# Edge counts of a four-layer graph network: place registers loaded by fours, and the narrow one-hots of twelve steps compared in one instruction

## Chip, cores and metric

One core of one Trainium2 chip runs the whole program in one launch. The metric is device time in microseconds (us): the median of three runs of the kernel before is 5613.37 us (5609.27 to 5640.14). One more run was recorded by the hardware profiler; every row below comes from it.

## The reference, cut to what matters

Four graph layers run one after the other on 3125 nodes with 64 features and the same 100,000 edges, which come sorted by `dst`: an attention layer (8 heads), two mean aggregations, an edge-weighted aggregation, and a second attention layer with a feed-forward part. The first two layers need, for every pair of nodes, nothing but how many edges join them, for instance:

```python
scores = leaky_relu(alpha_src[src] + alpha_dst[dst], 0.2)
att = exp(clip(scores, -2.0, 2.0))
att_sum = segment_sum(att, src, N)
out = segment_sum(h[dst] * (att / att_sum[src])[:, :, None], src, N)
...
msg_sum = segment_sum(x[src], dst, n)      # mean aggregation, twice
mean = msg_sum / maximum(deg, 1.0)[:, None]
```

Both sums over edges can be written as products with a dense table counts[dst, src], the number of edges from src to dst. The change lies wholly in the stage that builds this table.

## The kernel before

**Sizes.** The edges are cut into G = 800 groups of P = 125. The `dst` nodes are cut into V = 125 windows of D = 25 nodes. A step is one (group, window) pair that shares edges; there are KV = 800 + 125 - 1 = 924 steps, in order of window. For each edge of a step the stage `order_edges` has worked out `src_code` (the src's place, 0 to 124, inside its own block of 125 nodes) and `pair_code` (0 to 649: which of 26 columns per dst, 25 of them blocks of 125 src nodes, and which of the 25 dst nodes; a code outside marks an edge of another window).

**One step** (class `Count`). VectorE (DVE) makes two one-hot tables in bf16 by comparing an iota row with one value per partition: the wide one, `pair_hot`, 125 x 650 (line 484), and the narrow one, `src_hot`, 125 x 125 (line 485). TensorE (PE) multiplies them: 125 edges contracted, narrow one-hot as the weights, wide one-hot as the moving operand, in two halves of 325 columns (line 525), and adds onto a 125 x 650 fp32 table in PSUM. There are 12 places (UV = 12) for each one-hot; DVE may refill a place once PE has counted the step that used it (`count_ready`), PE may use it once `hot_ready` says so.

**One window.** Which PSUM table a step adds to is data: a window has some 7.4 steps on average and there are four PSUM places (SLOTS = 4) used in turn. The place of each step is in the row `fine.slot`, and the number of places that must have been cleared before a pair of steps may write is in `fine.turn` (one value per two steps). ScalarE (ACT) waits until a window is complete, copies 125 x 650 out (line 500), clears the place (line 503), and the SyncE queue (SP) writes the window to HBM in two DMAs (line 473), with DEEP = 6 windows in flight.

**What sets PE's order.** The PE program is straight-line. At the start of each round of 12 steps it loads registers from SBUF (`values`, line 460): twelve `slot` values in one instruction and six `turn` values in another. Then for each step it waits for `hot_ready`, for each second step it waits for `slot_free` against a `turn` register (line 523), and issues two matmuls, each preceded by a register operation that forms the PSUM address. 924 steps make 77 rounds.

Before the stage, PE and ACT compute score rows while DVE already makes the first 12 pairs of one-hots; after it comes a barrier, and the attention layer reads the table back from HBM. Elsewhere in the program (class `Unpack`, line 201) PE, ACT and DVE load registers four at a time (AT_LOAD = 4).

Of the kernel before, what the change touches and what calls it, by code (L numbers as in the profile page):

```python
# [21 lines left out]
BF16 = mybir.dt.bfloat16  # L22
F16 = mybir.dt.float16
I32 = mybir.dt.int32
ALU = mybir.AluOpType
# [4 lines left out]
P = 125  # L30
# [8 lines left out]
V = N // D  # L39
KV = G + V - 1  # L40
UV = 12
CW = 26 * D
FAR = 1.0e30
AT_ONCE = 2
# [6 lines left out]
SLOTS = 4  # L51
# [78 lines left out]
def over(ap, shape):  # L130
    return ap.to_broadcast(list(shape))
# [174 lines left out]
def order_edges(nc, m):  # L306


    with ExitStack() as stack:
# [25 lines left out]
        def _(dve):  # L335
# [37 lines left out]
            own(v.tensor_tensor(t.window_f[:, :], m.step_iota[:, 0:KV], group[:, :], ALU.subtract))  # L373
            own(v.tensor_scalar(first[:, :], t.window_f[0:P, :], float(CW), -MIDDLE, ALU.mult, ALU.add))

            own(v.tensor_scalar(row[:, 0:HALF], t.window_f[0:1, 1:KV:2], 1.0, None, ALU.add))
            own(v.tensor_copy(t.turn[:, :], row[:, 0:HALF]))
            own(v.tensor_scalar(row[:, :], t.window_f[0:1, :], 1.0 / SLOTS, None, ALU.mult))
            own(v.tensor_copy(t.slot[:, :], row[:, :]))
            own(v.tensor_copy(row[:, :], t.slot[:, :]))  # L380
# [56 lines left out]
class Count:  # L437
# [7 lines left out]
    def __init__(self, nc, s, m):  # L445
        self.nc, self.m = nc, m
        used = DEEP * CW + 3 * N
        hot = m.arena[0:P, used:used + UV * (CW + P) // 2].bitcast(BF16)
        self.pair_hot = hot[:, 0:UV * CW].rearrange("p (i c) -> p i c", i=UV)
        self.src_hot = hot[:, UV * CW:].rearrange("p (i c) -> p i c", i=UV)  # L450
        self.zeros = s.sb("zeros", [P, CW // 2], BF16)
        self.sum = [m.arena[0:P, i * CW:(i + 1) * CW].rearrange("p (a c) -> p a c", a=2) for i in range(DEEP)]
        self.ps = s.ps("count_ps", (128, SLOTS, 2, 512))
        self.sum_out = s.sems("sum_out", DEEP)
        self.blank, self.hot_ready, self.count_ready = s.sem("blank"), s.sem("hot_ready"), s.sem("count_ready")
        self.evicted, self.slot_free = s.sem("evicted"), s.sem("slot_free")

    def values(self, engine, table, k, n, most):

# [18 lines left out]
    def dve(self, dve):  # L478
        nc, m, v = self.nc, self.m, self.nc.vector

        for k in range(KV):
            if k >= UV:
                dve.wait_ge(self.count_ready, k - UV + 1)
            v.tensor_scalar(self.pair_hot[:, k % UV, :], m.code_iota[:, :], m.fine.pair_code[:, k:k + 1], None, ALU.is_equal)  # L484
            v.tensor_scalar(self.src_hot[:, k % UV, :], m.node_iota[:, :], m.fine.src_code[:, k:k + 1], None,  # L485
                            ALU.is_equal).then_inc(self.hot_ready, 1)

    def act(self, act):

# [15 lines left out]
    def pe(self, pe, tables):  # L505
        nc, m = self.nc, self.m

        pe.wait_ge(self.blank, 1)
        pe.wait_ge(tables.scores_taken, 1)
        pe.wait_ge(tables.rows_copied, 2 * tables.chunks)  # L510
        for i in range(SLOTS):
            for c in range(2):
                last = nc.tensor.matmul(self.ps[0:P, i, c, 0:CW // 2], self.zeros[:, 0:P], self.zeros[:, :],
                                        start=True, stop=True, skip_group_check=True)
            last.then_inc(self.slot_free, 1)

        for k in range(KV):
            if k % UV == 0:
                slots = self.values(mybir.EngineType.PE, m.fine.slot, k, UV, SLOTS - 1)
                turns = self.values(mybir.EngineType.PE, m.fine.turn, k // 2, UV // 2, V)  # L520
            pe.wait_ge(self.hot_ready, k + 1)
            if k % 2 == 0:
                pe.wait_ge(self.slot_free, turns[k % UV // 2])
            for c in range(2):
                last = nc.tensor.matmul(self.ps[0:P, bass.ds(slots[k % UV], 1), c, 0:CW // 2].rearrange("p a f -> p (a f)"),  # L525
                                        self.src_hot[:, k % UV, :], self.pair_hot[:, k % UV, c * (CW // 2):(c + 1) * (CW // 2)],
                                        start=False, stop=True, skip_group_check=True)
            last.then_inc(self.count_ready, 1)

# [1762 lines left out]
def program(nc, io, out):  # L2292
    m = Memory()
    with ExitStack() as stack:
# [29 lines left out]
        with ExitStack() as first:  # L2324
# [11 lines left out]
            with ExitStack() as held:  # L2336
                m.arena = held.enter_context(nc.sbuf_tensor("arena", [128, HELD * AT_ONCE * V // W * CW], F32))
                m.held = Counts(nc, held, m)
                with ExitStack() as layer0:
                    def layer0_sb(name, shape, dt=F32):  # L2340
                        return layer0.enter_context(nc.sbuf_tensor(name, shape, dt))
                    m.wt0, m.at0, m.merge = layer0_sb("wt0", [F, HF]), layer0_sb("at0", [F, 2 * H]), layer0_sb("merge", [F, H, F])
                    m.node_iota = layer0_sb("node_iota", [P, P], F16)
                    m.group_iota = layer0_sb("group_iota", [ROWS, RUNS])
                    m.far_past, m.far_left = layer0_sb("far_past", [P, W, H]), layer0_sb("far_left", [P, W, H])
                    with ExitStack() as early:
                        def early_sb(name, shape, dt=F32):
                            return early.enter_context(nc.sbuf_tensor(name, shape, dt))
                        m.src_rows, m.dst_rows = early_sb("src_rows", [ROWS, EACH], I32), early_sb("dst_rows", [ROWS, EACH], I32)
                        m.code_iota = early_sb("code_iota", [P, CW], F16)  # L2350
                        m.fine = Memory()
                        m.step_iota16 = early_sb("step_iota16", [ROWS, KV], F16)
                        m.fine.window_f = early_sb("fine_window_f", [128, KV])
                        m.fine.src_code, m.fine.pair_code = (early_sb(f"fine_{n}", [P, KV]) for n in ("src_code", "pair_code"))
                        m.fine.slot, m.fine.turn = (early_sb(f"fine_{n}", [1, k], I32) for n, k in (("slot", KV), ("turn", HALF)))
                        m.fine.counted = early_sb("fine_counted", [1, V], I32)
                        set_up(nc, m, io)
                        order_edges(nc, m)
                        count_and_tables(nc, m)
                    m.gathered = layer0_sb("gathered", [P, W, F])  # L2360
                    attend(nc, m, "l0")
                    finish_layer0(nc, m)
                    m.acc = m.sums
                count_sum(nc, m, "l1a", 0, with_tiles=True)
                with ExitStack() as extra:
                    m.held.grow(nc, extra)
                    finish_mean(nc, m, "l1a_end", m.sage1[:, :], m.rows[:, 0:F], "hidden")
                    count_sum(nc, m, "l1b", 1)
                finish_mean(nc, m, "l1b_end", m.sage2[:, :], m.rows[:, F:2 * F], "last")
# [41 lines left out]
```

## Time and profile before

| | |
|---|---|
| median of three runs | 5613.37 us |
| the profiled run, its own time | 5605.08 us |
| its span, first to last instruction | 5603.3 us |
| DVE busy over the span | 3211.7 us (57%) |
| PE matmul busy over the span | 3079.5 us (55%) |
| granted TensorE clock, mean of the span | 0.712 |
| count stage, first to last matmul of line 525 | 103.0 to 588.9 us |

Busy times overlap between engines, and a stage ends when its last engine does; so the share of an engine over the whole span does not say what the count stage waits for. Idle time is read from the rows of the stage itself: a row's bracket gives the idle time of its engine just before it and what ended it. "issue" stands for time in which the engine waited for nothing that the profile shows as work; loads of registers are such time, and they are listed only where one asks for their source line (engine names with a q, as PEldq, are the sequencer's own instructions).

### The profile page before, as it was taken

The page shows a single profiled execution, that of the slowest core. Times are in us where ns is not written, and L with a number is a line of the kernel's source. Part 1 is how long each engine was busy: PE and PEld are TensorE (multiplying, and loading weights), DVE is VectorE, ACT ScalarE, POOL GpSimd, SP SyncE. Part 2 cuts the span into 40 slices and gives each one's busy share as a digit, 9 for nine tenths or more (in the row PEclk, how much of TensorE's full clock was granted, in tenths as well). Part 3 has the DMA queues.
Part 4 walks back from the last instruction along what each step waited for, and adds up shares of the span by engine and source line. Part 5 has one row for each costly group of instructions (what it writes and reads, how often), then busy time and mean ns, then how long its engine had stood idle before and what let it go on. Part 6 is the DMA issues. An engine that isn't in the chain of part 4 may idle for free. (4 is left out here: it accounts for less than half of the span.)

```text
span 5603.3 us, 46575 instructions
## 1 busy us (share of the span) xinstructions
PE 3079.5 (55%) x11765; PEld 1927.7 (34%) x11765; DVE 3211.7 (57%) x5607; ACT 1827.1 (33%) x2737; POOL 1842.8 (33%) x1787
## 2 busy tenths in 40 slices
PE   5777688877777776885334432441101543433564
PEld 3555333322222222553223332441001433333552
DVE  6999799999999997102132111112211854556676
ACT  1333688888888885000000000000101111111200
POOL 0000222100000000001777777754775066665200
PEclk7888899999999998997555555555555555555556
DMA  1222666544444444984214222102111011111011
GB/s 38 83 85 85 170 186 191 162 118 120 119 120 123 118 116 112 211 181 99 48 40 98 45 48 44 43 17 37 31 27 29 15 37 32 37 31 30 4 42 32
DMA packets 381011, 448.82 MB, mean 80 GB/s; under 512 B 182902, under 2 KB 249365, under 8 KB 379839
## 3 DMA queue, kind: packets, MB, share of 16 engines
q1 hardware_dynamic: 328477, 390.50, 27.0%
q0 software_dynamic: 52288, 55.34, 5.1%
q8 instruction: 117, 1.92, 0.2%
q14 instruction: 129, 1.06, 0.1%
HBM read 351.39 MB, written 94.23 MB: 80 GB/s over the span
## 5 line engine op out<-in xcount | busy, mean ns | idle before, releaser
L889 PE MATMUL l_sum_ps<-arena,sums 125*65 125x500 f32 (+1 forms) x2600 | 1146.0, 580 | 295.8 <-DVE arena L783 272.1
L1808 POOL DMA_INDIRECT l_rows<-table,tile_src x782 | 772.1, 987 | 508.5 <-issue 229.6
L1219 POOL DMA_INDIRECT l_rows<-hidden_rows,tile_src x782 | 806.4, 1031 | 304.9 <-issue 233.9
L772 DVE SCALAR_TENSOR_TENSOR arena<-arena,far_past 125x750 f32<-125x750 f32 (+1 forms) x800 | 859.7, 1114 | 16.5 <-DMA arena<-score_rows 16.5
L1272 PE MATMUL l_acc_ps<-l_rows,l_hot 128*125 x1612 | 389.6, 388 | 718.6 <-issue 683.3
L818 ACT ACTIVATE arena<-arena,far_left 125x750 f32<-125x750 f32 (+1 forms) x800 | 713.0, 939 | 186.0 <-DVE arena L772 186.0
L783 DVE SCALAR_TENSOR_TENSOR arena<-arena,l_turned 125x1500 f32<-125x1500 f32 (+1 forms) x400 | 711.6, 1779 | 47.9 <-ACT arena L823 47.3
L2002 PE MATMUL l_sum_ps<-l_rows,l_hot 128*128 x1962 | 482.4, 425 | 439.5 <-issue 302.1
L889 PEld LDWEIGHTS l_sum_ps<-arena,sums 125*65 125x65 f32 x2600 | 331.6, 138 | 1045.0 <-issue 534.6
L1272 PEld LDWEIGHTS l_acc_ps<-l_rows,l_hot 128*125 128x125 f32 x1612 | 367.1, 313 | 742.2 <-issue 740.3
L2002 PEld LDWEIGHTS l_sum_ps<-l_rows,l_hot 128*128 128x128 f32 x1962 | 437.7, 327 | 483.0 <-issue 480.7
L823 ACT ACTIVATE arena<-arena 125x1500 f32<-125x1500 f32 (+1 forms) x400 | 596.7, 1492 | 0.0
L1923 DVE SCALAR_TENSOR_TENSOR acc<-acc,l_factor,l_sum_ps 128x65 f32 x981 | 275.9, 281 | 549.3 <-DMA found_rows<-l_w_last_i 344.9
L525 PE MATMUL l0tab_count_ps<-arena 125*125 125x325 bf16 x1848 | 348.8, 353 | 140.2 <-DVE arena L485 136.3
L484 DVE TENSOR_SCALAR arena<-code_iota,fine_pair_code 125x650 bf16<-125x650 f16 x924 | 356.6, 386 | 54.5 <-PE l0tab_count_ps L525 54.3
L1311 ACT ACTIVATE l_end_dense_sb<-l_end_ps_t 128x500 f32<-128x500 f32 (+1 forms) x7 | 3.7, 542 | 1168.9 <-PE l_end_ps_t L1297 1168.9
L744 POOL TENSOR_TENSOR gathered<-gathered,arena 125x384 f32<-125x384 f32 (+1 forms) x12 | 28.4, 2363 | 1068.0 <-DVE arena L796 1068.0
L1236 DVE TENSOR_TENSOR l_rows<-l_rows,l_attr 128x512 f32<-128x512 f32 x98 | 68.0, 694 | 517.2 <-DMA l_rows<-hidden_rows,tile_src 482.4
L525 PEld LDWEIGHTS l0tab_count_ps<-arena 125*125 125x125 bf16 x1848 | 282.3, 157 | 207.0 <-issue 161.2
L2049 ACT ACTIVATE l_step_att<-l_att 128x8 f32 x981 | 176.9, 208 | 469.7 <-issue 393.7
L1230 DVE TENSOR_TENSOR l_hot<-tile_rel,node_row 128x1000 f32<-128x1000 f32 x101 | 120.5, 1194 | 338.9 <-DMA arena<-counts 305.4
L485 DVE TENSOR_SCALAR arena<-node_iota,fine_src_code 125x125 bf16<-125x125 f16 x924 | 230.8, 250 | 0.0
(464 smaller groups left out, 2738.3 us busy)
## 6 DMA issues: line engine op xcount, KB each, us to landing
l_turned<-turned_counts SPq DMA_DIRECT2D x225, 328.1 KB
arena<-counts SPq DMA_DIRECT2D x17, 2843.8 KB
counts<-arena SPq DMA_DIRECT2D x125, 284.4 KB
l_turned<-turned_counts SPq DMA_DIRECT2D x75, 382.8 KB
l_attr<-edge_attr_in SPq DMA_DIRECT2D x97, 256.0 KB
arena<-counts SPq DMA_DIRECT2D x75, 328.1 KB
turned_counts<-l_turned SPq DMA_DIRECT2D x75, 328.1 KB
arena<-score_rows SPq DMA_DIRECT2D x24, 732.4 KB
```

The lines of the kernel that those rows point to most:

```text
L484: v.tensor_scalar(self.pair_hot[:, k % UV, :], m.code_iota[:, :], m.fine.pair_code[:, k:k + 1], None, ALU.is_equal)
L525: last = nc.tensor.matmul(self.ps[0:P, bass.ds(slots[k % UV], 1), c, 0:CW // 2].rearrange("p a f -> p (a f)"), self.src_hot[:, k % UV, :], ...
L772: last = v.scalar_tensor_tensor(scores(k)[:, i, :], rows[:, 1, i, :], m.far_past[:, w, h:h + 1], rows[:, 0, i, :], ALU.add, ALU.max)
L783: v.scalar_tensor_tensor(scores(k), scores(k), LOWEST, over(turned_counts(k).unsqueeze(1), (P, PAIR, n * P)), ALU.max, ALU.mult).then_inc( ...
L818: last = nc.scalar.activation(here, here, ACT.Relu, scale=-1.0, bias=m.far_left[:, w, h:h + 1])
L823: nc.scalar.activation(scores(k), scores(k), ACT.Exp, scale=-1.0).then_inc(raised, 1)
L889: last = nc.tensor.matmul(sum_ps[0:F + 1, c, 0:hi - lo], h_one[:, w, :], z[k % ZS][:, lo:hi], start=(w == 0), stop=(w == W - 1))
L1219: pool.indirect_dma_start(rows[:, b % RING, t, :], None, m.hidden_rows[:, :], bass.IndirectOffsetOnAxis(ap=m.tile_src[:, k:k + 1], axis=0) ...
L1272: last = nc.tensor.matmul(nodes[:, bass.ds(window, 1), :].rearrange("p a f -> p (a f)"), hot[r % HOTS][:, j, :], flat[:, bass.ds(place, 1) ...
L1808: pool.indirect_dma_start(rows[:, t % RING3, :], None, m.table3[:, :], bass.IndirectOffsetOnAxis(ap=m.tile_src[:, t:t + 1], axis=0)).then_ ...
L1923: v.scalar_tensor_tensor(window, window, factor[:, k:k + 1], sum_ps[g % 4][:, i * (F + 1):(i + 1) * (F + 1)], ALU.mult, ALU.add).then_inc( ...
L2002: last = nc.tensor.matmul(sum_ps[g % 4][:, i * (F + 1):(i + 1) * (F + 1)], hot[g % 3][:, i, :, :].rearrange("p h j -> p (h j)"), rows[:, b ...
```

## The change

- The PE program loads four `slot` values at each fourth step (one instruction), and four `turn` values at each sixteenth (three at the last). `fine.turn` holds one value per four steps, that of the last of the four, and PE waits for `slot_free` once per four steps, ahead of them.
- DVE no longer compares the narrow one-hot step by step. One two-operand comparison makes those of twelve steps: a table `node_step` (node number, repeated for twelve steps, fp16, made once) against twelve `src_code` values, now kept in fp16 and read again for each node. The result lies node by node with the twelve steps side by side, so the 125 weights of one step are 12 elements (24 bytes) apart. There is room for three such groups (NARROW = 36 steps); group g + 1 is compared in the middle of group g.
- PE waits once per twelve steps for `narrow_ready`. The wide one-hots and the matmuls' shapes and number stay.

```diff
--- before.py
+++ after.py
@@ -39,6 +39,7 @@
 V = N // D
 KV = G + V - 1
 UV = 12
+NARROW = 3 * UV
 CW = 26 * D
 FAR = 1.0e30
 AT_ONCE = 2
@@ -373,8 +374,8 @@
             own(v.tensor_tensor(t.window_f[:, :], m.step_iota[:, 0:KV], group[:, :], ALU.subtract))
             own(v.tensor_scalar(first[:, :], t.window_f[0:P, :], float(CW), -MIDDLE, ALU.mult, ALU.add))
 
-            own(v.tensor_scalar(row[:, 0:HALF], t.window_f[0:1, 1:KV:2], 1.0, None, ALU.add))
-            own(v.tensor_copy(t.turn[:, :], row[:, 0:HALF]))
+            own(v.tensor_scalar(row[:, 0:KV // AT_LOAD], t.window_f[0:1, AT_LOAD - 1:KV:AT_LOAD], 1.0, None, ALU.add))
+            own(v.tensor_copy(t.turn[:, :], row[:, 0:KV // AT_LOAD]))
             own(v.tensor_scalar(row[:, :], t.window_f[0:1, :], 1.0 / SLOTS, None, ALU.mult))
             own(v.tensor_copy(t.slot[:, :], row[:, :]))
             own(v.tensor_copy(row[:, :], t.slot[:, :]))
@@ -445,15 +446,18 @@
     def __init__(self, nc, s, m):
         self.nc, self.m = nc, m
         used = DEEP * CW + 3 * N
-        hot = m.arena[0:P, used:used + UV * (CW + P) // 2].bitcast(BF16)
+        hot = m.arena[0:P, used:used + (UV * CW + NARROW * P) // 2].bitcast(BF16)
         self.pair_hot = hot[:, 0:UV * CW].rearrange("p (i c) -> p i c", i=UV)
-        self.src_hot = hot[:, UV * CW:].rearrange("p (i c) -> p i c", i=UV)
+        self.src_hot = hot[:, UV * CW:].rearrange("p (a c i) -> p a i c", a=NARROW // UV, i=UV)
+        self.node_step = s.sb("node_step", [P, P, UV], F16)
+        self.node_step_ready = s.sem("node_step_ready")
         self.zeros = s.sb("zeros", [P, CW // 2], BF16)
         self.sum = [m.arena[0:P, i * CW:(i + 1) * CW].rearrange("p (a c) -> p a c", a=2) for i in range(DEEP)]
         self.ps = s.ps("count_ps", (128, SLOTS, 2, 512))
         self.sum_out = s.sems("sum_out", DEEP)
         self.blank, self.hot_ready, self.count_ready = s.sem("blank"), s.sem("hot_ready"), s.sem("count_ready")
         self.evicted, self.slot_free = s.sem("evicted"), s.sem("slot_free")
+        self.narrow_ready = s.sem("narrow_ready")
 
     def values(self, engine, table, k, n, most):
 
@@ -478,12 +482,21 @@
     def dve(self, dve):
         nc, m, v = self.nc, self.m, self.nc.vector
 
+        v.tensor_copy(self.node_step[:, :, :], over(m.node_iota[:, :].unsqueeze(2), (P, P, UV))).then_inc(self.node_step_ready, 1)
+        dve.wait_ge(self.node_step_ready, 1)
+
+        def narrow(a):
+            v.tensor_tensor(self.src_hot[:, a * UV % NARROW // UV, :, :].rearrange("p i c -> p c i"), self.node_step[:, :, :],
+                            over(m.fine.src_code[:, a * UV:(a + 1) * UV].unsqueeze(1), (P, P, UV)), ALU.is_equal
+                            ).then_inc(self.narrow_ready, 1)
+        narrow(0)
         for k in range(KV):
             if k >= UV:
                 dve.wait_ge(self.count_ready, k - UV + 1)
-            v.tensor_scalar(self.pair_hot[:, k % UV, :], m.code_iota[:, :], m.fine.pair_code[:, k:k + 1], None, ALU.is_equal)
-            v.tensor_scalar(self.src_hot[:, k % UV, :], m.node_iota[:, :], m.fine.src_code[:, k:k + 1], None,
+            v.tensor_scalar(self.pair_hot[:, k % UV, :], m.code_iota[:, :], m.fine.pair_code[:, k:k + 1], None,
                             ALU.is_equal).then_inc(self.hot_ready, 1)
+            if k % UV == UV // 2 and k // UV + 1 < KV // UV:
+                narrow(k // UV + 1)
 
     def act(self, act):
 
@@ -515,15 +528,18 @@
             last.then_inc(self.slot_free, 1)
 
         for k in range(KV):
+            if k % AT_LOAD == 0:
+                slots = self.values(mybir.EngineType.PE, m.fine.slot, k, AT_LOAD, SLOTS - 1)
+            if k % AT_LOAD ** 2 == 0:
+                turns = self.values(mybir.EngineType.PE, m.fine.turn, k // AT_LOAD, min(AT_LOAD, (KV - k) // AT_LOAD), V)
+            if k % AT_LOAD == 0:
+                pe.wait_ge(self.slot_free, turns[k // AT_LOAD % AT_LOAD])
             if k % UV == 0:
-                slots = self.values(mybir.EngineType.PE, m.fine.slot, k, UV, SLOTS - 1)
-                turns = self.values(mybir.EngineType.PE, m.fine.turn, k // 2, UV // 2, V)
+                pe.wait_ge(self.narrow_ready, k // UV + 1)
             pe.wait_ge(self.hot_ready, k + 1)
-            if k % 2 == 0:
-                pe.wait_ge(self.slot_free, turns[k % UV // 2])
             for c in range(2):
-                last = nc.tensor.matmul(self.ps[0:P, bass.ds(slots[k % UV], 1), c, 0:CW // 2].rearrange("p a f -> p (a f)"),
-                                        self.src_hot[:, k % UV, :], self.pair_hot[:, k % UV, c * (CW // 2):(c + 1) * (CW // 2)],
+                last = nc.tensor.matmul(self.ps[0:P, bass.ds(slots[k % AT_LOAD], 1), c, 0:CW // 2].rearrange("p a f -> p (a f)"),
+                                        self.src_hot[:, k % NARROW // UV, k % UV, :], self.pair_hot[:, k % UV, c * (CW // 2):(c + 1) * (CW // 2)],
                                         start=False, stop=True, skip_group_check=True)
             last.then_inc(self.count_ready, 1)
 
@@ -2351,8 +2367,8 @@
                         m.fine = Memory()
                         m.step_iota16 = early_sb("step_iota16", [ROWS, KV], F16)
                         m.fine.window_f = early_sb("fine_window_f", [128, KV])
-                        m.fine.src_code, m.fine.pair_code = (early_sb(f"fine_{n}", [P, KV]) for n in ("src_code", "pair_code"))
-                        m.fine.slot, m.fine.turn = (early_sb(f"fine_{n}", [1, k], I32) for n, k in (("slot", KV), ("turn", HALF)))
+                        m.fine.src_code, m.fine.pair_code = early_sb("fine_src_code", [P, KV], F16), early_sb("fine_pair_code", [P, KV])
+                        m.fine.slot, m.fine.turn = (early_sb(f"fine_{n}", [1, k], I32) for n, k in (("slot", KV), ("turn", KV // AT_LOAD)))
                         m.fine.counted = early_sb("fine_counted", [1, V], I32)
                         set_up(nc, m, io)
                         order_edges(nc, m)
```

## Rows read from the trace of the kernel before

**Rows 1.** Waits, count stage: engine, line, waited-for, us, times, longest

```profile
PEld l0tab_count_ps L525 <- issue: 161.2, 78, 3.5
PE l0tab_count_ps L525 <- DVE arena L485: 136.3, 65, 3.2
DVE arena L484 <- PE l0tab_count_ps L525: 54.3, 53, 11.3
```

**Rows 2.** Busy time by stretch: length, PE, PEld, DVE, ACT, POOL, clock, DMA, GB/s

```profile
103.00:589.00 486.00, 348.56 (x1848) 282.23 (x1848) 439.10 (x1824) 174.93 (x245) 0.00 (x0) 0.86 0.27 84
750.00:2150.00 1400.00, 1108.31 (x3101) 392.17 (x3100) 1356.38 (x1122) 1200.33 (x1166) 137.57 (x96) 0.98 0.48 134
```

**Rows 3.** Timeline, PE and weight loads: start, us, line, shape, count, [idle before]

```profile
301.29 3.85 PE L525 MATMUL l0tab_count_ps<-arena 125*125 125x325 bf16 x24 [2.82 <-DVE arena L485]
...
307.43 0.77 PE L525 MATMUL l0tab_count_ps<-arena 125*125 125x325 bf16 x4 [2.28 <-DVE arena L485]
...
301.29 3.59 PEld L525 LDWEIGHTS l0tab_count_ps<-arena 125*125 125x125 bf16 x24 [3.07 <-issue]
...
301.29 0.38 PEld L525 LDWEIGHTS l0tab_count_ps<-arena 125*125 125x125 bf16 x3 [3.07 <-issue]
...
173.92 6.41 PE L525 MATMUL l0tab_count_ps<-arena 125*125 125x325 bf16 x23 [3.20 <-DVE arena L485]
```

**Rows 4.** Register loads by line, ns min/median/max: 297:308, then whole span

```profile
L460 PEldq TENSOR_LOAD <-fine_slot x2: 851/1046/1242, 298.1 to 304.8; - x2
L460 PEldq TENSOR_LOAD <-fine_turn x2: 1062/1534/2005, 299.0 to 306.1; - x2
...
L460 PEldq TENSOR_LOAD <-fine_slot x77: 843/868/3384, 97.8 to 582.9; - x77
L460 PEldq TENSOR_LOAD <-fine_turn x77: 818/1438/2218, 101.3 to 584.2; - x77
L460 ACTq TENSOR_LOAD <-fine_counted x32: 291/308/510, 96.7 to 587.1; - x32
...
L201 PEldq TENSOR_LOAD <-words x246: 14/333/700, 3985.4 to 5399.0; - x123
```

**Rows 5.** Timeline, DVE: start, us, engine, line, shape, [idle before]

```profile
304.14 0.39 DVE L484 TENSOR_SCALAR arena<-code_iota,fine_pair_code 125x650 bf16<-125x650 f16 x1
304.44 0.25 DVE L485 TENSOR_SCALAR arena<-node_iota,fine_src_code 125x125 bf16<-125x125 f16 x1
304.60 0.39 DVE L484 TENSOR_SCALAR arena<-code_iota,fine_pair_code 125x650 bf16<-125x650 f16 x1
...
25.05 3.05 DVE L348 TENSOR_SCALAR arena<-step_iota,order_finish 100x924 f16<-100x924 f16 x8
```

**Rows 6.** DVE instructions by line, ns min/median/max: one operand, then two

```profile
L242 DVE TENSOR_SCALAR h<-h x4: 993/993/994, 70.8 to 3805.7; 125x1600 f32<-125x1600 f32 x4
...
L348 DVE TENSOR_SCALAR arena<-step_iota,order_finish x8: 453/454/461, 25.1 to 27.7; 100x924 f16<-100x924 f16 x8
...
L228 DVE TENSOR_TENSOR l0tab_cen<-x,l0tab_mean x1: 1826/1826/1826, 61.7 to 61.7; 125x1600 f32<-125x1600 f32 x1
```

**Rows 7.** Weight loads by line, ns min/median/max: far apart, then side by side

```profile
L1966 PEld LDWEIGHTS l_far_ps<-ident,l_rows x104: 132/173/279, 3954.8 to 5202.2; 128*64 128x64 f32 x96, 128*14 128x14 f32 x8
...
L2184 PEld LDWEIGHTS l3end_heads_t<-ident,acc x200: 108/173/178, 5411.1 to 5523.6; 128*64 128x64 f32 x100
```

**Rows 8.** ACT and SP queue by line, ns min/median/max

```profile
L500 ACT ACTIVATE arena<-l0tab_count_ps x125: 712/713/716, 107.1 to 589.2; 125x650 f32<-125x650 f32 x125
...
L503 ACT ACTIVATE l0tab_count_ps<-l0tab_zeros x121: 715/715/717, 107.8 to 575.7; 125x650 f32<-125x650 bf16 x121
...
L473 SPq DMA_DIRECT2D counts<-arena x250: 298/309/1482, 107.8 to 590.3; - x125
```

**Rows 9.** Timeline at the stage's start: start, us, engine, line, count, [idle before]

```profile
102.96 5.90 PEld L525 LDWEIGHTS l0tab_count_ps<-arena 125*125 125x125 bf16 x24 [3.27 <-issue]
...
103.81 0.39 DVE L484 TENSOR_SCALAR arena<-code_iota,fine_pair_code 125x650 bf16<-125x650 f16 x1 [11.28 <-PE l0tab_count_ps L525]
```

## Prediction

> **What bounds the kernel now.** I read the waits of the count stage first, then its busy time by stretch, then one round on the timeline, and last the sequencer's own instructions by source line. The stage takes 486.0 us from 103 to 589 us, 8.7% of the span [rows 2]; 77 rounds of 12 steps, so 6.31 us a round. No engine is full in it: DVE is busy 439 of 486 us, PE's matmuls 349, ACT 175 [rows 2]. The waits name two things: PE's weight loads stood still 161.2 us for "issue", in 78 places, that is once a round, while DVE waited 54.3 us for PE, in 53 places [rows 1]. The 136 us put down to DVE on the matmul rows are the same gaps seen from the other side: one round shows it. From 301.29 us PE issues 24 matmuls; the next come at 307.43, 6.14 us later [rows 3]. Its two register loads begin at 304.8 and 306.1 us and take 1.24 and 1.06 us [rows 4]; in the round before they began at 298.1 and 299.0 and took 0.85 and 2.01, and the weight load at 301.29 stood idle 3.07 us [rows 3, 4]. DVE could not have helped: with all twelve places full it waits for PE's first step. So the round is PE's: load the registers, then issue 24 matmuls, and nothing on PE lies beside the loads.
>
> The terms of a round at full clock come from these rows. Three weight loads in a row span 0.38 us, the last one 0.13 of it, so one matmul is issued each (0.38 - 0.133)/2 = 0.1235 us. All 24 weight loads span 3.59 us: 3.46 up to the start of the last, less 23 x 0.1235 = 2.84, leaves 0.62 for the five waits of line 523 in between, 0.124 each. Around the loads: from the start of a last weight load to the next first one are 3.07 + 0.13 = 3.20 us, of which 2.86 are the two loads; the other 0.34 are a wait and a matmul's issue (0.247) and some 0.05 for each load; with 0.36 in the other round I take 0.06 a load. At half clock a round's matmuls are the array's: 23 of them span 6.41 us, 0.27 each, 6.5 for 24 [rows 3].
>
> **Register loads by fours and one wait per four steps.** Per round go the 12-value load (median 0.868 us) and the six-value load (median 1.438, least 0.818), some 2.3 us by medians, plus 0.12 [rows 4]. In come 3 loads of `slot` and 0.75 of `turn`, each of four values. PE's loads of four in another stage take 0.333 us (median of 246), and ACT's loads of four in this very stage 0.308 (median of 32, longest 0.51) [rows 4]. 3.75 x (0.333 + 0.06) = 1.47 us. Of six waits three remain, 0.37 us; the new wait for the narrow one-hots adds 0.12. Issue stays: 24 x 0.1235 = 2.96. PE's round: 2.96 + 0.37 + 0.12 + 1.47 = 4.93 us. The bounds: if all loads hid behind queued matmuls the round would be 3.46; with a load of four at what the shortest six-value load took here (0.818 + 0.06) it is 2.96 + 0.49 + 3.29 = 6.74. I take 4.93, since two engines agree on a load of four. Queued behind a blocked `slot_free` wait are up to eight matmuls; it asks for a place given back some three windows, 22 steps, earlier, so it should stay satisfied.
>
> The Trainium skill speaks against loading in small pieces: Runtime: NRT & Kernel Launch (section Instruction fetch mechanics) gives about 200 ns for each register. By it four would cost 0.8 us, a round 3.45 + 3.75 x 0.86 = 6.7, and the stage would lengthen by some 30 us. The trace disagrees: four take 0.333 us, twelve 0.868 [rows 4].
>
> **The narrow one-hots.** DVE now starts a wide comparison 0.30 us before the narrow one and a narrow one 0.16 before the next wide one [rows 5]; 12 x 0.46 = 5.52 us a round. Two wide ones in a row are not in the trace, but eight comparisons of 924 elements span 3.05 us at 0.454 each, so the next starts 0.08 us before the end of one [rows 5, 6]; 0.385 - 0.085 = 0.30 holds for wide after wide. The comparison of 1500 elements with two 16-bit operands has no row. Two-operand work on fp32 takes 1.826 us for 1600 elements, 1.72 for 1500. One-operand work takes 0.993 us for 1600 fp32 and 0.454 for 924 16-bit elements; less some 0.16 and 0.21 of fixed time that is 0.52 and 0.26 ns an element, so 16 bits halve it [rows 6]. Bounds: 0.6 us (at the one-operand 16-bit rate) and 1.72; I take half the fp32 rate, 0.94, or 0.85 start to start. DVE's round is then 12 x 0.30 + 0.85 = 4.45 us, between 4.1 and 5.2. It stays under PE's 4.93 unless near the upper end, and twelve places are enough to ride over the lump in the middle of a group. DVE's new work at the start (making `node_step` and the first group, under 3.5 us) lies in the 11.28 us that it waited there [rows 9]: nothing; without that cover, 3.5 us once.
>
> **Weights 24 bytes apart.** Weight loads whose weights lie 292 bytes apart (line 1966) have a median of 173 ns, like those side by side (line 2184) for the same 64 columns [rows 7]. Both are mostly from the slow level of the clock, so at the fast level the cost isn't shown. I take nothing. A load may even grow to 4.93/24 = 0.205 us a matmul before it is seen. The Trainium skill speaks against this layout as well: SBUF — State Buffer (the note on 16-byte cachelines) says that each access in a new line pays a penalty, with eight bf16 as the free distance; twelve is beyond it. It gives no size; the row shows none.
>
> **The clock.** In the stage the granted clock is 0.86 of full, so 28% of it at 1.2 GHz, where PE stood idle 2.5 to 3.5 us in each round; from 750 to 2150 us, with PE busy 79% of the time in small gaps, it is 0.98 [rows 2, 3]. The idle pieces shrink to 0.4 to 0.8 us, so I take 10% at the low level: 1/(0.9/4.93 + 0.1/6.5) = 5.05 us a round.
>
> **Others.** ACT needs 2 x 0.71 us and a quarter of 0.31 a window, 1.5 of the 3.1 us that a window will last; SP's two issues are under 1 us a window in most cases [rows 4, 8]. Edits of `order_edges` are a few tenths of a microsecond. At the start the first loads end earlier, 3.27 us of idle before 102.96 [rows 9]: a gain of 2 us (0 to 2.6).
>
> **Sum.** 77 x 5.05 = 389 us in place of 486: 97 us, with the start 99 us. The profiled run of 5605.1 us (1.8 outside its span) would be 5506; it lies 8.3 below the median, so the median of 5613.4 becomes 5514.
>
> **Rivals.**
> - PE's round under 4.9 us, with loads hidden in part behind the queue: DVE's 4.45 then binds, 343 us, 5468 at the least. For it: at half clock the array is slower than issue, so matmuls queue up and a load can pass beside them. Against: at full clock PE's weight loads start evenly at 0.1235 us apart, and the gap after them is the full length of the loads [rows 3, 4].
> - The narrow comparison at one element per cycle, 1.72 us: DVE's round 3.6 + 1.63 = 5.23, 403 us, 5528. For: the fp32 rows. Against: 16-bit rows at double rate.
> - The clock swings as now: 1/(0.72/4.93 + 0.28/6.5) = 5.28, 407 us, 5532; at the low level throughout 6.5, 500 us, 5625, no change.
> - Slower: on PE in this stage a load costs by the instruction and not by the value. For: six and twelve values have nearly the same least time, 0.818 and 0.843. Then 6.74 a round, 519 us, less 2: 5644. It decides from (6.31 - 3.45)/3.75 - 0.06 = 0.70 us a load.
> - Strided weights at double the recorded 0.133 us, with nothing hidden: 24 x 0.266 = 6.4, 491 us, 5617, no change; it decides from 0.263. Three times would be 9.6, 250 us slower.
> - The change doesn't do what it says: loads by fours cost nearly what they cost now. No change.
>
> **Chances.** Forecast 0.65; lower 0.05; one element per cycle 0.10; clock as now 0.06, low throughout 0.02; slower loads 0.07; strided weights 0.04, half of it slower; no effect 0.01. A difference of 0.5% (28 us) is about what a measurement of this kernel can tell. Faster 0.65 + 0.05 + 0.10 + 0.06 = 0.86, same 0.05, slower 0.09. The range takes in the first four cases: 5488 (a round of 4.7) to 5560.
>
> **What would show it.** Right: rounds of the 24 matmuls near 5 us, PE idle pieces of 0.4 to 0.9 us three or four times a round, register loads of four near 0.33 us, a comparison of 125 x 1500 of 0.94 us 77 times, clock over 0.93 in the stage, DVE waiting for PE. Wrong: loads of four over 0.7 us, weight loads over 0.2 us at full clock, or PE waiting for DVE with a comparison of 1.7 us. All later stages should only shift.

## The result, and the profile after

The changed kernel's median is 5537.5 us (5530.4 to 5544.8, four runs) against 5617.7 (5609.3 to 5640.1, four runs): ratio 0.9853, 95% interval 0.9824 to 0.9881, 80 us less. A second set of runs (e5 below) gave 5550.0 against 5628.8, ratio 0.9863 (0.9844 to 0.9882), 79 us less. The forecast, made from a median of 5613.4 for the kernel before, was 5514 in a range of 5488 to 5560; 99 us less were expected.

Lines of the page of the changed kernel (part 1, and two rows of the 40 slices):

```profile
PE 3147.2 (57%) x11765; PEld 2053.9 (37%) x11765; DVE 3153.6 (57%) x4761; ACT 1829.5 (33%) x2737; POOL 1839.6 (33%) x1787
...
PE   6997888787877777893253424250002533434564
...
PEclk8998999999999998996565555555555555555556
```

Its busy time by stretch, columns as in [rows 2]; first the count stage (to 505 us, where it reached 589 before), then the neighbour sums of the mean aggregations and the last attention layer, which the change doesn't touch:

```profile
103.00:505.00 402.00, 401.56 (x1839) 401.34 (x1837) 378.75 (x983) 175.59 (x246) 0.00 (x0) 1.00 0.33 102
...
2135.00:2507.00 372.00, 326.06 (x1488) 206.62 (x1488) 36.59 (x73) 13.29 (x33) 1.73 (x3) 0.94 0.90 181
...
3789.00:5347.00 1558.00, 539.76 (x2276) 478.42 (x2276) 751.36 (x1859) 233.15 (x1036) 818.42 (x828) 0.50 0.14 26
```

PE and its weight loads are now busy in all 402 us, at a granted clock of 1.00; before it was 349 of 486 us at 0.86 [rows 2]. The waits of the stage, columns as in [rows 1], agree: the 161 us in which weight loads stood still are gone, and of the stage itself nearly nothing waits but ACT:

```profile
ACT arena L513 <- PE l0tab_count_ps L541: 228.8, 125, 7.5
...
DVE arena L496 <- PE l0tab_count_ps L541: 8.3, 4, 7.9
```

The stage by source line (duration ns min/median/max, first and last start). Line 541 was 525, 489 is the new comparison, 496 the wide one, 464 the register loads [rows 4, 6]:

```profile
L541 PEldq FUSED_REGOPS  x1848: 46/46/51, 99.9 to 501.1; - x185
L541 PEld LDWEIGHTS l0tab_count_ps<-arena x1848: 291/312/322, 100.0 to 504.0; 125*125 125x125 bf16 x185
L541 PE MATMUL l0tab_count_ps<-arena x1848: 329/382/637, 100.0 to 504.2; 125*125 125x325 bf16 x185
...
L464 PEldq TENSOR_LOAD <-fine_slot x231: 327/332/978, 96.9 to 499.7; - x116
L464 PEldq TENSOR_LOAD <-fine_turn x58: 325/329/2258, 97.5 to 496.2; - x58
...
L489 DVE TENSOR_TENSOR arena<-l0tab_node_step,fine_src_code x77: 930/933/941, 87.7 to 492.2; 125x1500 bf16<-125x1500 f16 x77
```

From the first to the last matmul are 404.2 us, 5.25 a round; it was 485.9. A weight load is recorded with 312 ns where it had 133 [rows 3]. And the last register operation starts at 501.1 us, 3.1 us ahead of the last matmul (before: 588.7 and 588.9): PE's sequencer, the part that executes waits, register loads and issues, has run ahead, and what it has issued stands in the queue as work for the array, the part that multiplies. On the timeline the matmuls follow without a gap, 0.218 us apart (6.49 less the last one's 0.38 is 6.11 us for 28):

```profile
299.78 6.49 PE L541 MATMUL l0tab_count_ps<-arena 125*125 125x325 bf16 x29
```

Where the time went: the stage's first weight load starts 3.0 us earlier (99.99 against 102.96 [rows 9]), the stage is 81.7 us shorter, and the attention layer behind it starts 84.7 us earlier. The two profiled spans differ by only 60.2 us, as two later stages that the change doesn't touch were longer in this one: the second and third stretch above, 372 and 1558 us, were 360 and 1542. The profiled run of before was 13 us under its median and this one 7 over; the medians, 80 us apart, show the stage's gain.

### The profile page after: what moved, and what is told of

The parts are those of the page before. It is cut to its first block and busy times, and to the rows that moved or that the text cites. A ratio compares the mean times of both kernels' runs of the same rounds, so it can differ in the third digit from the quotient of the medians.

```text
span 5543.1 us, 45633 instructions
## 1 busy us (share of the span) xinstructions
PE 3147.2 (57%) x11765; PEld 2053.9 (37%) x11765; DVE 3153.6 (57%) x4761; ACT 1829.5 (33%) x2737; POOL 1839.6 (33%) x1787
## 5 line engine op out<-in xcount | busy, mean ns | idle before, releaser
L1288 PE MATMUL l_acc_ps<-l_rows,l_hot 128*125 x1612 | 387.8, 390 | 717.8 <-issue 700.6
L541 PE MATMUL l0tab_count_ps<-arena 125*125 125x325 bf16 x1848 | 404.6, 383 | 0.7 <-PE l0tab_count_ps L526 0.7
L541 PEld LDWEIGHTS l0tab_count_ps<-arena 125*125 125x125 bf16 x1848 | 404.4, 313 | 1.2 <-issue 1.2
L496 DVE TENSOR_SCALAR arena<-code_iota,fine_pair_code 125x650 bf16<-125x650 f16 x924 | 326.9, 390 | 26.4 <-PE l0tab_count_ps L541 8.3
L769 POOL COPY arena<-arena 125x750 f32<-125x750 f32 (+1 forms) x100 | 123.6, 1237 | 306.3 <-PE l_count_ps L894 238.4
```

Source lines behind the costliest of these rows:

```text
L541: last = nc.tensor.matmul(self.ps[0:P, bass.ds(slots[k % AT_LOAD], 1), c, 0:CW // 2].rearrange("p a f -> p (a f)"), self.src_hot[:, k % NA ...
L1288: last = nc.tensor.matmul(nodes[:, bass.ds(window, 1), :].rearrange("p a f -> p (a f)"), hot[r % HOTS][:, j, :], flat[:, bass.ds(place, 1) ...
```

## Experiments

e1 to e4 ran on another chip, on which the kernel before takes 5333.9 us (5328.2 to 5340.3) and not 5617; the last attention layer is some 185 us shorter in the runs there. The edge-weighted aggregation is some 90 us shorter there. So between chips only the count stage is compared (time from its first to its last matmul), and ratios go by runs of the kernel before on the experiment's own chip. The stage of the kernel before was profiled on one chip only; its 485.9 us stand for the others too, and the ratios bear that out (e3: 62 us of the stage, 63 us by the medians). Rows of an experiment are of its main matmul line and its line of register loads; means of register loads are worked out from all those of PE in the stage, and a distance between matmuls is the median over the stage.

**e1: weights 8 bytes apart.**

```diff
-NARROW = 3 * UV
+NU, NARROW = 4, 36
-... "p (a c i) -> p a i c", a=NARROW // UV, i=UV
+... "p (a c i) -> p a i c", a=NARROW // NU, i=NU
-            if k % UV == UV // 2 and k // UV + 1 < KV // UV:
-                narrow(k // UV + 1)
+            if k % NU == NU // 2 and (k // NU + 1) * NU < KV:
+                narrow(k // NU + 1)
```

The same replacement stands in `narrow`, in `node_step` and in PE's wait for `narrow_ready`, which now comes every four steps.

> The changed kernel with the narrow one-hots compared by four steps, so that a step's weights lie 8 bytes apart and not 24. In the changed kernel a matmul starts each 0.218 us (before: 0.142 at full clock) and PE is never idle, 24 x 0.218 = 5.23 us a round. Theory A (what counts is how many of the weights share a 16-byte piece of a partition; two or more are enough): loads are as quick as side by side, the array falls back to 0.142 and the round is bound by issue and register loads, 24 x 0.1235 + 3 x 0.124 + 3.75 x 0.39 = 4.80 us, with DVE's 12 x 0.30 + 3 x 0.33 = 4.6 below it: stage 370 us, 33 us less than changed. Theory B (any gap between weights costs the full price): 0.218 a matmul as before, stage 403 us, no difference. Theory C (the 0.218 has nothing to do with the layout but with DVE's and ACT's traffic): no difference either, or slower with DVE's three comparisons a round.

Measured: 5261.2 us, ratio 0.986 (0.9844 to 0.9877), stage 415.6 us.

```profile
L542 PEld LDWEIGHTS l0tab_count_ps<-arena x1848: 190/192/231, 102.7 to 518.2; 125*125 125x125 bf16 x185
L542 PE MATMUL l0tab_count_ps<-arena x1848: 300/303/538, 102.7 to 518.3; 125*125 125x325 bf16 x185
...
PEld l0tab_count_ps L542 <- issue: 145.5, 225, 1.3
...
301.69 1.39 PE L542 MATMUL l0tab_count_ps<-arena 125*125 125x325 bf16 x8 [0.17 <-DVE arena L497]
303.23 1.39 PE L542 MATMUL l0tab_count_ps<-arena 125*125 125x325 bf16 x8 [0.15 <-issue]
```

The matmuls are back at 0.142 us apart, with DVE and ACT about as busy as in the changed kernel (e8 shows the row): theories B and C fall, the 0.218 is the distance between weights. But the stage is 46 us over what A gave, and 11 over the changed kernel's. PE now stops after each eight matmuls for its register loads (225 pieces, 145.5 us). Their median is 0.333 us as expected, their mean 0.467: 2.96 + 0.37 + 3.75 x (0.467 + 0.06) = 5.3 us a round, 5.40 measured. So the forecast's load was the median of a skewed set.

The row's "<-DVE" is not to be taken at its word. Matched step by step in the trace, a wide one-hot of e1 is finished at least 3.0 us before its first matmul starts: PE waits behind its register loads, and the row names the last semaphore that was due.

**e2: 16 bytes apart.** As e1 with NU = 8 and NARROW = 32.

> As e1, by eight steps: weights 16 bytes apart, each in a 16-byte piece of its own. Theory A: as slow as 24 bytes, 0.218 a matmul, stage 403 us. Theory D (only a gap beyond 16 bytes costs): 0.142 a matmul, stage about 370 us. A price in proportion to the distance: about 0.17 to 0.19 a matmul, hidden under issue, stage about 370 to 390 us.

Measured: 5269.4 us (one run), stage 423.4 us, matmuls 0.228 apart.

```profile
L543 PEld LDWEIGHTS l0tab_count_ps<-arena x1848: 302/325/330, 100.5 to 523.7; 125*125 125x125 bf16 x185
```

As slow as 24 bytes, even a little slower (0.228 against 0.218). Theory D falls, and so does a price in proportion to the distance, which would have given 0.17 to 0.19; A holds in kind. The stage is 20 us longer than A's 403, which took the 0.218 for both.

**e3: loads and waits alone.** The kernel before with the register loads, the wait and the `fine.turn` of the change, everything else as before.

```diff
-            if k % UV == 0:
-                slots = self.values(..., m.fine.slot, k, UV, SLOTS - 1)
-                turns = self.values(..., m.fine.turn, k // 2, UV // 2, V)
+            if k % AT_LOAD == 0:
+                slots = self.values(..., m.fine.slot, k, AT_LOAD, SLOTS - 1)
...
-            if k % 2 == 0:
-                pe.wait_ge(self.slot_free, turns[k % UV // 2])
+            if k % AT_LOAD == 0:
+                pe.wait_ge(self.slot_free, turns[k // AT_LOAD % AT_LOAD])
```

> The kernel before with the register loads by four and one wait per four steps, narrow one-hots step by step as before. If PE's round was the loads, it falls to 4.9 us and DVE's 12 x 0.46 = 5.52 us takes over: stage 425 us against 486, 61 us saved, DVE never waiting for long. Rival: the loads of four cost more where the array has no backlog (0.7 us and up): round 6.3 us and no gain.

Measured: 5270.9 us, ratio 0.9889 (0.9873 to 0.9906), stage 423.7 us; on the timeline DVE starts a step each 0.46 us without a pause.

```profile
300.33 0.39 DVE L484 TENSOR_SCALAR arena<-code_iota,fine_pair_code 125x650 bf16<-125x650 f16 x1
300.63 0.26 DVE L485 TENSOR_SCALAR arena<-node_iota,fine_src_code 125x125 bf16<-125x125 f16 x1
300.79 0.39 DVE L484 TENSOR_SCALAR arena<-code_iota,fine_pair_code 125x650 bf16<-125x650 f16 x1
...
PE l0tab_count_ps L526 <- DVE arena L485: 92.7, 181, 1.3
```

62 of the 82 us of the stage come from this half of the change; then DVE binds at 5.50 us a round, as its 12 x 0.46 said. Here the row's "<-DVE" is real: a narrow one-hot is finished as little as 0.14 us before its matmul (median 0.82), where the kernel before has at least 2.1.

**e4: the narrow one-hots alone.** The changed kernel with the loads and waits of before (e3's edit the other way round).

> The changed kernel with the twelve- and six-value loads and the wait per two steps of before. If loads pass beside queued matmuls, the round is issue plus loads, 24 x 0.1235 + 6 x 0.124 + 2.3 + 0.2 = 6.2 us: stage 477 us, about 10 us less than before. If the array stands still while they load, 5.23 + 2.3 = 7.5 us: stage 580 us, 90 us more than before.

Measured: 5332.0 us, ratio 0.9998 (0.9988 to 1.0007), stage 482.2 us, 6.26 a round.

```profile
PEld l0tab_count_ps L540 <- issue: 66.6, 63, 3.3
...
L540 PEld LDWEIGHTS l0tab_count_ps<-arena x1848: 291/312/323, 104.8 to 586.8; 125*125 125x125 bf16 x185
```

No gain beyond noise, and 4 us of the stage where 10 were expected: loads pass beside queued matmuls ("issue" falls from 161 to 67 us [rows 1] although the loads are the same, 1.21 us in the mean and 1.24 before), but the sequencer's own 6.2 us bind. The 580 us of the other case didn't come. The second half of the change is worth something only behind the first.

**e5: the changed kernel again**, beside e6 to e8.

> The changed kernel once more, beside e6 to e8. If its stage is the array's (a matmul each 0.218 us because the weights lie 24 bytes apart), it takes 1848 x 0.218 = 403 us on any chip, with the register loads hidden behind queued matmuls. Rival: the stage follows the register loads and differs from chip to chip.

Measured: 5550.0 us, ratio 0.9863 (0.9844 to 0.9882), stage 404.2 us, the same to 0.1 us; mean load 0.390 us both times.

**e6: 12 bytes apart.** As e1 with NU = 6.

> The narrow one-hots by six steps: weights 12 bytes apart, a 16-byte piece holds one or two. Loads of weights: 133 ns side by side, 192 at 8 bytes (e1), 312 to 325 at 24 and 16 bytes. If the price goes by pieces touched (1.33 weights each), a load is some 260 ns and a matmul about 0.17 us, 4.1 us a round: hidden under issue and register loads, stage like e1's 416 us or a little less, since the slower array has matmuls queued that cover long register loads. If 12 bytes cost like 16, 0.22 a matmul: 403 to 423 us.

Measured: 5565.8 us, ratio 0.9885 (0.9865 to 0.9905), stage 423.5 us.

```profile
L542 PEld LDWEIGHTS l0tab_count_ps<-arena x1848: 246/270/275, 103.3 to 526.7; 125*125 125x125 bf16 x185
...
PEld l0tab_count_ps L542 <- issue: 74.4, 137, 1.2
```

A weight load of 270 ns and 0.174 us between matmuls: the price that was worked out from pieces touched. At 12 bytes 125 weights touch 94 pieces of 16 bytes, at 16 and 24 bytes 125: 1.85, 1.82 and 1.74 ns a piece; at 8 bytes they touch 63, which by the same estimate is 0.11 us a matmul and hidden under the 0.142. The stage was to be no longer than e1's and is 8 us longer. The sequencer has one wait more a round: by six, the waits for the narrow one-hots come at steps 0 and 6 and that for a place at 0, 4 and 8, four in all; by four both come at 0, 4 and 8 and are one instruction each. The trace has 308 wait instructions of this line in e6 (`L540 PEldq EVENT_SEMAPHORE  x308`), 231 in e1 and in the changed kernel, that is 4 and 3 a round. 2.96 + 4 x 0.124 + 3.75 x 0.527 = 5.43 us, 5.50 measured.

**e7: e6 with one turn value and one place wait per twelve steps.**

```diff
-            if k % AT_LOAD ** 2 == 0:
-                turns = self.values(..., m.fine.turn, k // AT_LOAD, min(AT_LOAD, (KV - k) // AT_LOAD), V)
-            if k % AT_LOAD == 0:
-                pe.wait_ge(self.slot_free, turns[k // AT_LOAD % AT_LOAD])
+            if k % (AT_LOAD * UV) == 0:
+                turns = self.values(..., m.fine.turn, k // UV, min(AT_LOAD, (KV - k) // UV), V)
+            if k % UV == 0:
+                pe.wait_ge(self.slot_free, turns[k // UV % AT_LOAD])
```

> e6 with one turn value and one wait for a cleared place per twelve steps: 0.5 fewer register loads and one wait fewer a round. If issue and loads bind (e1: 5.40 us a round), it gains 0.5 x 0.5 + 0.12 = 0.4 us a round, 29 us of the stage against e6. If the array binds at 12 bytes, nothing. Rival: the wait over twelve steps now blocks, because a place twelve steps ahead is not yet cleared: a round longer by up to 1.5 us, slower than e6.

Measured: 5532.8 us, ratio 0.9835 (0.9807 to 0.9862), stage 388.5 us: 35 us under e6 and 16 under e5, the changed kernel on the same chip (17 us by the medians). Issue and loads did bind e6, and the longer wait doesn't block. It is two waits a round fewer, not one (154 wait instructions): by the sum of e1, with the mean load of each run, 38 us.

```profile
L542 PEld LDWEIGHTS l0tab_count_ps<-arena x1848: 246/270/276, 101.6 to 490.0; 125*125 125x125 bf16 x185
...
PEld l0tab_count_ps L542 <- issue: 45.3, 87, 1.1
```

**e8: e1 with each window written twice**, the second time to a tensor that nothing reads.

```diff
-                sp.dma_start(row[lo:hi, :], ...).then_inc(self.sum_out[v % DEEP], 16)
+                for to in (row, self.again[v, :, :]):
+                    sp.dma_start(to[lo:hi, :], ...).then_inc(self.sum_out[v % DEEP], 16)
```

> e1 with every window written twice to HBM (the second time to a tensor that nothing reads). In e1 loads of four registers take 0.333 us in the median but 0.47 in the mean; the long ones, 0.6 to 1.3 us, stand where three times as many packets of the window writes start. If the writes cause them, doubling the writes about doubles the share of long loads: mean near 0.6, 3.75 x 0.13 = 0.5 us a round, stage 450 us against 416. If something else does (instruction fetch, ACT's own loads), mean and stage stay as in e1.

Measured: 5616.9 us (one run), stage 462.1 us. Stretch and loads, first of e1, then of e8:

```profile
105.00:500.00 395.00, 307.73 (x1757) 253.65 (x1756) 348.80 (x1098) 169.55 (x238) 0.00 (x0) 1.00 0.32 98
```

```profile
L465 PEldq TENSOR_LOAD <-fine_slot x231: 327/334/959, 99.6 to 516.6; - x116
```

```profile
105.00:500.00 395.00, 285.58 (x1573) 235.66 (x1572) 317.32 (x986) 151.82 (x213) 0.00 (x0) 0.96 0.56 177
```

```profile
L466 PEldq TENSOR_LOAD <-fine_slot x231: 327/529/1652, 97.3 to 560.9; - x116
```

Twice the DMA traffic (98 to 177 GB/s), a median of 0.529 in place of 0.334, a mean of 0.63 in place of 0.47: register loads of PE grow with the window writes. (The two medians are of the `slot` loads, the means of all.) By the formula 0.16 x 3.75 = 0.6 us a round, 5.9; the stage has 6.0. ACT's loads don't show it (308 ns in both), and why is open.

The traces settle it further, load by load. From 105 to 480 us the twelve profiled runs with loads of four have 1262 PE loads during whose first 0.33 us no packet of the queue that writes the windows starts: the longest takes 0.339 us. Of the 1744 others 46% take over 0.5 us. So every long load of four there stands beside window writes. Whether it is their reads of SBUF, their writes to HBM or something of SP's issue isn't separated.

**e9: e7 with 24 places for the wide one-hots** (`pair_hot` indexed by k % 24, DVE waiting 24 steps back).

> e7 with 24 places for the wide one-hots and not 12. In e7 (stage 388 us, 5.05 us a round) PE waited 25 us for DVE and DVE 17 us for PE, in turn, around long register loads. With more places DVE runs on during a long load; left is PE's issue, 24 x 0.1235 + 2 x 0.124 + 3.25 x 0.53 = 4.93 us: stage 380 us, 8 less than e7. Rival: DVE's own 12 x 0.30 + 2 x 0.46 = 4.5 us isn't the reason for those waits, and nothing changes.

Measured: 5524.9 us, ratio 0.983 (0.9811 to 0.9849), stage 387.8 us. The rival held: 0.7 us. The waits of PE for DVE in e7 weren't a matter of places, nor were they waits for DVE: matched step by step, the wide one-hot is finished at least 2.8 us before its matmul in e7, and 7.5 in e9.

**e10: e9 by four steps.**

> e9 with the narrow one-hots by four steps: weights 8 bytes apart, 0.142 us a matmul in place of 0.174, but one more wait and one more comparison a round (DVE 4.6 us). If a somewhat slow array helps, since matmuls queue up and cover long register loads, this one is slower than e9 by 0.1 to 0.2 us a round, some 10 us. If array speed only hurts, it is equal or faster.

Measured: 5564.2 us (one run), stage 400.1 us, 12 more than e9. It is the direction expected, but the one wait more (3 against 2) is 77 x 0.124 = 9.5 us by itself, and longer loads (mean 0.482 against 0.472) add 77 x 3.25 x 0.01 = 2.5; that a slower array helps isn't shown.

**e11: e7's edit on the changed kernel.**

> The changed kernel with one wait and turn value per twelve steps, the edit that took 35 us from the stage between e6 and e7. If the changed kernel's stage is bound by the array (24 bytes between weights, 0.218 us a matmul), it gains nothing: 404 us. If issue and register loads bind it, some 30 us less, 374 us.

Measured: 5554.9 us (one run), stage 403.9 us. No gain, where the same edit took 35 us between e6 and e7.

```profile
105.00:485.00 380.00, 380.00 (x1743) 380.00 (x1742) 363.22 (x944) 168.57 (x236) 0.00 (x0) 1.00 0.33 102
```

The array is busy to the last 0.01 us. The changed kernel's stage is the array's.

**e12: twelve at once, weights side by side.**

```diff
-... "p (a c i) -> p a i c"
+... "p (a i c) -> p a i c"
-            v.tensor_tensor(self.src_hot[:, a ...].rearrange("p i c -> p c i"), self.node_step[:, :, :],
-                            over(m.fine.src_code[:, ...].unsqueeze(1), (P, P, UV)), ALU.is_equal
+            v.tensor_tensor(self.src_hot[:, a ...], over(m.node_iota[:, :].unsqueeze(1), (P, UV, P)),
+                            over(m.fine.src_code[:, ...].unsqueeze(2), (P, UV, P)), ALU.is_equal
```

> The changed kernel with the twelve narrow one-hots compared in the other order, step by step, so that a step's weights lie side by side and the src code is the operand that stays the same along a row. The array falls back to 0.142 us a matmul. The comparison of 1500 elements goes from 0.933 us to about 1.72 if such an operand takes DVE to one element a cycle: DVE 12 x 0.30 + 1.63 = 5.23 us a round beside PE's 5.3 (issue plus loads at a mean of 0.47): stage 410 to 425 us, no better than the changed kernel's 404, though nothing waits for the array. If the comparison stays at 0.93, 415 us as e1.

Measured: 5571.7 us, ratio 0.9907 (0.9889 to 0.9925), stage 415.1 us.

```profile
L489 DVE TENSOR_TENSOR arena<-node_iota,fine_src_code x77: 1701/1714/1722, 88.9 to 503.8; 125x1500 bf16<-125x1500 f16 x77
...
L541 PEld LDWEIGHTS l0tab_count_ps<-arena x1848: 132/133/231, 101.2 to 516.2; 125*125 125x125 bf16 x185
```

The comparison takes 1.714 us, 0.933 the other way; the weight load is back at 133 ns. The layout of the change buys DVE 0.78 us a round and costs the array 24 x 0.076 = 1.8. In e12 the sequencer binds again (5.3 us by the sum of e1, 5.39 measured). DVE's 5.2 comes near it but doesn't bind: each wide one-hot is finished 1.69 us or more before its matmul. In the changed kernel the array (5.23) binds alone, and its stage comes out 11 us ahead.

## Why the prediction was right, and where it was off

**The bound of before** (register loads in PE's program): right. e3 shortens them alone and gets 62 us of the stage, up to DVE's 5.50 us a round; 5.52 was the reading from [rows 5].

**A load of four, 0.333 us**: right in the median (0.332), wrong as a term of the sum, which wants the mean: 0.390 in the changed kernel, 0.467 in e1, 0.63 with the writes doubled (e8). The group of [rows 4] showed medians with a longest of 0.70, and the 0.82 to 2.2 us of the old loads were a sign that something stretched them. Per round it is 3.75 x 0.057 = 0.2 us here.

**The waits**: three, not four, a round (231 instructions in the trace). The wait for the narrow one-hots falls together with the one for a place and is one instruction with two conditions; 0.12 us too much in the sum. With both corrections the sequencer's round is 2.96 + 0.37 + 3.75 x 0.45 = 5.02 us, and the runs bound by it (e1, e6, e7, e10, e12) lie 0.1 above what the same sum gives for them; that 0.1 is unexplained.

**Weights 24 bytes apart, taken at nothing**: this step failed, and it sets the time. The rival was stated with its point: seen from 0.205 us a matmul, a loss from 0.263. It came to 0.218, just over the first: 24 x 0.218 = 5.23 us a round against the 4.93 forecast, 77 x 0.30 = 23 us. The row compared loads at the low level of the clock and was no evidence at the high one, as the forecast itself said before it took nothing.

SBUF — State Buffer (note on 16-byte cachelines), of the Trainium skill, pointed the right way: it asks for at least two hits in a line of 16 bytes. The runs agree: with two weights in 16 bytes (8 apart) matmuls keep their 0.142 us, with 1.33 it is 0.174, with one 0.228. The free distance of eight bf16 that the same note gives doesn't agree: eight elements (16 bytes) cost the 0.228, and already at four a load is recorded with 192 ns, hidden behind the 0.142 us of its matmul.

**Loads hidden behind the queue**: written down as the rival for a faster stage, it happened, but as a consequence of the slower array. That is why the array's 5.23 stands alone and isn't added to the loads. It isn't by itself why e1, with quick weights, is slower than the changed kernel: with e1's mean load of 0.467 the changed kernel's sequencer would need 5.31 us by the sum, more than the array. The loads are also shorter where the array binds (mean 0.390, 0.390, 0.394 and 0.428 in the changed kernel, e5, e2 and e11; 0.457 to 0.482 in e1, e3, e6, e7, e9, e10 and e12). Why is open.

**The clock**: better than taken. The low level was given 10% of the stage; 103 to 505 us has 1.00. That alone was 0.12 us a round, 9 us, and offsets part of the miss: 5.25 measured for 5.05 forecast.

**The comparison of 1500 elements, 0.94 us**: 0.933. **DVE under PE**: right; each wide one-hot is finished at least 3.4 us before its matmul, and DVE waits for its places. **Start, 2 us**: the stage's start moved by 3.0, of which 1.0 came from the stages ahead.

**Sum.** 77 x (5.25 - 5.05) = 15 us of the 19 between forecast gain (99) and measured (80); the rest, 4 us, is inside the spread of the runs. That the time fell into the range is in part luck: what binds the stage had been taken at nothing, 0.30 us a round too little, and the clock gave back 0.12. The slower cases didn't come: a load of four takes 0.33 us without traffic beside it, not 0.82.

The Trainium skill, Runtime: NRT & Kernel Launch (section Instruction fetch mechanics), has 200 ns a register, by which four would cost an estimated 0.8 us; 289 of them have a median of 0.33 here. The page speaks of registers loaded from HBM, and these rows lie in SBUF. Nor does a price by the register speak against small pieces, as the forecast had it: it prices the 18 values a round of before at 3.6 us and the 15 of the change at 3.0, a gain, where the old loads took 2.48 us and the new ones 1.46.

## What to carry to other kernels

Price a stage at each engine's own pace before adding gaps: once the gap goes, the next pace is what is left, and here three were within 15% of each other (array 5.23, sequencer 5.0, DVE 4.5 us a round), so each further edit moved only until it met the next (e7 gained 35 us where the sequencer bound, e11 none where the array did). When an operand's layout is changed for the engine that writes it, look at the engine that reads it, at the clock level at which it will run. Take the mean, not the median, of a wait that is paid in series. And before a wait row is believed that names another engine, look how long that engine's result had been ready: in e1, e7 and e12 the rows put 21 to 85 us down to DVE, whose results were 1.69 us and more ahead.

The best version run is e9 (5524.9 us, ratio 0.983). e7, with fewer edits, is 8 us above it by medians taken beside different runs of the kernel before, and 0.7 us by the stage.

## What the runs showed of the hardware that I had not expected

- Weight loads of 125 bf16 columns at full clock, by distance between weights, as recorded and as spacing of matmuls of 325 columns: 2 bytes 133 ns and 0.142 us; 8 bytes 192 and 0.142; 12 bytes 270 and 0.174; 16 bytes 325 and 0.228; 24 bytes 312 and 0.218. The 2-byte distance is that of the kernel before and of e12. That 16 is dearer than 24 is unexplained.
- PE's loads of four registers are stretched beside window writes: mean 0.47 us at 98 GB/s (e1), 0.63 at 177 (e8, one run), least 0.33 in both. With no packet of that queue starting in their first 0.33 us, 1262 of 1262 took at most 0.339 us. ACT's loads of the same size stay at 0.31. In the changed kernel, at 102 GB/s, the mean was only 0.39; why loads beside a full queue of matmuls are hit less often wasn't tried.
- A two-operand comparison of 16-bit data takes 0.933 us for 1500 elements, 0.543 for 750 (e6) and 0.411 for 500 (e1), that is 0.52 ns an element, if the repeated operand is a row that is read again. It takes 1.714 us for 1500 if that operand stays the same along a row (e12).
- A wait of PE on a semaphore costs its sequencer an estimated 0.12 us (from [rows 3]; the sums built on it come out 0.1 us a round short); two conditions at one point are one instruction (231 in the changed kernel, 308 in e6, 154 in e7).
